# Token tiles transposed by DMA as 16-bit planes in a gated cross-attention and feed-forward kernel

## The reference

```python
x = x + tanh(g_xattn) * xattn(layernorm(x), ctx_768, mask)     # x: (2, 2048, 512), ctx: (2, 77, 384)
x = x + tanh(g_ffn) * ffn(layernorm(x))

def xattn(x, context, mask):       # 16 heads of 32
    q, k, v = x @ Wq, context @ Wk, context @ Wv
    attn = softmax(where(mask, q k^T * 32**-0.5, -max))
    return (attn @ v) @ Wo

def ffn(x):                        # int8 fake quantisation, hidden size 1408
    xq = fake_quant(x)             # one scale from max |x| over the whole tensor
    h = fake_quant(silu(xq @ q(w_gate)^T) * (xq @ q(w_up)^T))
    return h @ q(w_down)^T
```

## Time and profile before

| | |
|---|---|
| median of 3 runs | 651.23 us (651.05 to 651.66) |
| profiled execution | 651.6 us, span of its instructions 649.6 us |
| mean granted TensorE clock | 0.994 |
| TensorE busy | 629.0 us (97%) |
| VectorE busy | 505.3 us (78%) |
| ScalarE busy | 319.8 us (49%) |
| GpSimd busy | 174.5 us (27%) |
| first `scores` of slot 3 / of slot 28 | 60.0 us / 347.4 us after the span's start |

### The profile page before, as it was taken

How to read it: one execution, slowest core, us unless ns; L and a number is a source line. 1 busy time by engine, 2 the same in 40 slices (tenths; PEclk the granted TensorE clock), 3 DMA queues, 4 the chain that set the end, 5 groups by cost and what they waited for, 6 DMA issues and landing times. The chain is left out here.

```text
span 649.6 us, 12819 instructions
## 1 busy us (share of the span) xinstructions
PE 629.0 (97%) x3987; PEld 478.6 (74%) x4008; DVE 505.3 (78%) x954; ACT 319.8 (49%) x488; POOL 174.5 (27%) x392
## 2 busy tenths in 40 slices
PE   8969999999999999999999997899999999899997
PEld 6769999999999999999999997444444444344544
DVE  6686878788787887888888766688888888876764
ACT  4354544445444554544544432555555554365653
POOL 7121223223232222212212111111111110047775
PEclk9999999999999999999999999899999999999999
DMA  8639111101111011011112000058465110089723
GB/s 308 189 95 318 47 28 26 49 24 48 24 29 44 25 48 25 28 52 62 29 47 68 18 7 0 18 174 192 161 210 202 31 28 17 0 291 413 292 105 128
DMA packets 59861, 63.32 MB, mean 97 GB/s; under 512 B 39571, under 2 KB 42029, under 8 KB 59821
## 3 DMA queue, kind: packets, MB, share of 16 engines
q1 hardware_dynamic: 54915, 46.03, 23.7%
q10 hardware_dynamic: 4906, 16.78, 7.0%
HBM read 32.48 MB, written 21.36 MB: 83 GB/s over the span
## 5 line engine op out<-in xcount | busy, mean ns | idle before, releaser
L633 DVE TENSOR_REDUCE sb_smax<-ps_s 128x8 f32<-128x616 f32 x64 | 51.1, 799 | 59.4 <-PE ps_s L926 59.0
L1231 ACT ACTIVATE sb_silu<-ps_g,sb_sgu 128x512 f32<-128x512 f32 x88 | 60.5, 687 | 72.1 <-PE ps_g L1318 43.8
L1318 PE MATMUL ps_g<-sb_xqT,sb_wgu 128*128 128x512 bf16 x344 | 89.3, 379 | 1.0 <-DVE sb_xqT L1274 0.6
L1318 PE MATMUL ps_u<-sb_xqT,sb_wgu 128*128 128x512 bf16 x346 | 89.4, 379 | 0.3
L527 ACT COPY sb_pT<-ps_p 128x512 f32<-128x512 f32 (+1 forms) x96 | 46.5, 520 | 71.5 <-PE ps_p L937 71.5
L1289 DVE SCALAR_TENSOR_TENSOR sb_h<-ps_u,sb_sgu,sb_silu 128x512 f32<-128x512 f32 (+1 forms) x88 | 66.1, 751 | 19.4 <-PE ps_u L1318 18.8
L948 PE MATMUL ps_o<-sb_vblk,sb_pT 128*128 (+4 forms) x640 | 79.0, 270 | 1.2 <-ACT sb_pT L527 1.2
L948 PEld LDWEIGHTS ps_o<-sb_vblk,sb_pT 128*128 128x128 f32 (+1 forms) x640 | 76.8, 191 | 1.8 <-ACT sb_pT L527 1.4
L881 PE MATMUL ps_q<-sb_xT_hi,sb_wq_hi 128*128 128x256 f32 x256 | 78.0, 305 | 0.0
L882 PE MATMUL ps_q<-sb_xT_lo,sb_wq_hi 128*128 128x256 f32 x256 | 72.6, 284 | 0.0
L883 PE MATMUL ps_q<-sb_xT_hi,sb_wq_lo 128*128 128x256 f32 x256 | 72.6, 284 | 0.0
(11 more groups left out here) (212 smaller groups left out, 1351.8 us busy)
## 6 DMA issues: line engine op xcount, KB each, us to landing
h_spill<-sb_h SPq DMA_DIRECT2D x4, 2816.0 KB, 8.9
sb_h<-h_spill ACTq DMA_DIRECT2D x16, 704.0 KB, 7.5
out_dram<-sb_wgu SPq DMA_DIRECT2D x31, 256.0 KB, 2.1
sb_x<-in_x_dram ACTq DMA_DIRECT2D x1, 4096.0 KB, 16.8
sb_w_in<-in_L_ffn_w_gate_dram SPq DMA_DIRECT2D x11, 256.0 KB, 2.6
sb_w_in<-in_L_ffn_w_up_dram SPq DMA_DIRECT2D x11, 256.0 KB, 2.6
sb_x<-in_x_dram SPq DMA_DIRECT2D x2, 1024.0 KB, 14.7
sb_x<-in_x_dram SPq DMA_DIRECT2D x2, 512.0 KB, 5.3
```

Source lines behind the costliest of these rows:

```text
L633: dve.tensor_reduce(smax[:, half, :].rearrange("p (g h) -> p g h", g=2), half_scores(), X, ALU.max).then_inc(v_max, 1)
L1231: act.activation(silu[(j * KI + i) % 2][:, :, :].rearrange("p t n -> p (t n)"), p_g[(j * KI + i) % 2][:, :], ACT.Silu, scale=sgu[:, i:i + ...
L1318: last = pe.matmul(banks[(j * KI + i) % 2][:, :], wgu[:, what, k, i * P:(i + 1) * P], xqT[j][:, k, :], start=(k == 0), stop=(k == KD - 1))
```

## The change

For tiles 4 to 31 TensorE no longer transposes the token tile. The fp32 tile `xn` is seen as pairs of 16-bit halves. GpSimd copies it to `xpl` as two planes, all low halves and then all high halves (`x_split`); SP transposes the 128 x 1,024 plane tile by DMA back into `xn` (`planes_transposed`); ScalarE joins the halves into fp32 values in `xpl` and copies those to `xT_hi` (`x_join`); GpSimd writes `xpl - xT_hi` to `xT_lo` (`x_low`). Tiles 0 to 3 keep the old way. `xpl` takes the room of `xabs`; the absolute values of tiles 0 to 23 are written to the PSUM tile `p_y` in place of it, so `project` waits for their reduction, and that reduction moves ahead of the second score subtraction. `outputs_norm(n - 1, 1)` comes after two waits that stood behind it. `DIRECT` is 4, `PLANES_FREE` is 28.

```diff
 # SP
+                    def planes_transposed(n):
+                        sp.wait_ge(g_xpl, n - DIRECT + 1)
+                        sp.dma_start_transpose(xn_u[:, :].rearrange("p (c n) -> p c n", n=P),
+                                               xpl_u[:, :]).then_inc(d_xT, 16)
...
                     values_spread(0, spread)
+                    planes_transposed(DIRECT)
                     rows(1)
                     for w in range(2, NW):
                         rows_transposed(w - 2)
+                        planes_transposed(w + DIRECT - 1)
                         rows(w)
...
                     down_rows(0)
+                    planes_transposed(NW + DIRECT)
                     for r in range(KD):
+                        if WD0 + 2 * r + 1 + DIRECT < NT:
+                            planes_transposed(WD0 + 2 * r + 1 + DIRECT)
                         for q in range(WC - 1):
                             down_stored(r, q)
                         if r + 1 < KD:
                             down_rows(r + 1)
+                        if WD0 + 2 * r + 2 + DIRECT < NT:
+                            planes_transposed(WD0 + 2 * r + 2 + DIRECT)
                         down_stored(r, WC - 1)
 # GpSimd
+                    def x_split():
+                        pool.tensor_copy(xpl_planes, xn_pairs).then_inc(g_xpl, 1)
...
+                        if split:
+                            wait(pool, a_xn, n)
+                            wait(pool, v_xlo, n - 1)
+                        else:
+                            wait(pool, a_xn, n - 1)
                         pool.tensor_tensor(ve[:, :], mv[:, 1:2], eps[:, :], ALU.add).then_inc(g_self, 1)
                         pool.tensor_tensor(nmean[:, :], mv[:, 0:1], minus[:, :], ALU.mult).then_inc(g_self, 1)
+                        if split:
+                            x_split()
...
+                        if runs(n + DIRECT, NT):
+                            x_low(n + DIRECT, t)
+
+                    def x_low(n, t):
+                        wait(pool, a_xhi, n + 1)
+                        wait(pool, t_q, n - t % 2 - 2)
+                        cols = slice(t % 2 * P, (t % 2 + 1) * P)
+                        pool.tensor_tensor(xT_lo[t // 2][:, :, cols], xpl_T, xT_hi[t // 2][:, :, cols].bitcast(F32),
+                                           ALU.subtract).then_inc(v_xlo, 1)
 # ScalarE
+                    def x_join(n, t):
+                        wait(act, d_xT, (n - DIRECT) * 16 + 16)
+                        act.copy(xpl_pairs, xn_planes).then_inc(a_xpl, 1)
+                        wait(act, a_xpl, n - DIRECT + 1)
+                        wait(act, t_q, n - t % 2 - 2)
+                        act.copy(xT_hi[t // 2][:, :, t % 2 * P:(t % 2 + 1) * P], xpl_T).then_inc(a_xhi, 1)
...
-                        if runs(n + 4, NT):
-                            x_part(n + 4, t)
+                        if runs(n + DIRECT, NT):
+                            x_join(n + DIRECT, t)
 # VectorE
                         down_part(n, 1)
+                        if runs(n - 4, NT):
+                            wait(dve, a_abs, n - 3)
+                            dve.tensor_reduce(xmax[:, span(n - 4)], xabs(n - 4), X, ALU.max).then_inc(v_xmax, 1)
                         if runs(n, NT):
                             scores_sub(n, t, 1)
...
-                        if runs(n + 4, NT):
-                            x_part(n + 4, t)
 # TensorE
                         wait(pe, v_x1, m)
+                        if not isinstance(m, int) or m < PLANES_FREE - 2:
+                            wait(pe, v_xmax, m)
...
-                        if runs(n + 4, NT):
-                            wait(pe, v_olo, n - 1)
-                            x_transpose(n + 4)
```

More of the change, by code:

```diff
@@ L11 @@
 U8 = mybir.dt.uint8
+U16 = mybir.dt.uint16
 ACT = mybir.ActivationFunctionType
@@ L63, in wd_step @@
     return (r, k) if 0 <= r < KD else (None, None)
+DIRECT = 4
+PLANES_FREE = NT - DIRECT
 CHUNKS = [(0, 4), (4, 8), (8, 2 * KB)]
@@ L129, in flamingo_block @@
                 sg_1 = sb("sg_1", [P, 2])
-                xn = sb("xn", [P, D])
+                xn_u = sb("xn", [P, 2 * D], U16)
+                xn = xn_u[:, :].bitcast(F32)
                 prob = [sb(f"prob{i}", [P, 2, HW]) for i in range(2)]
@@ L141, in flamingo_block @@
                 ends_n = sb("ends_n", [P, 2, 2])
-                xabs = sb("xabs", [P, D])
+                xpl_u = sb("xpl", [P, 2 * D], U16)
+                xpl = xpl_u[:, :].bitcast(F32)
                 mv1 = [sb(f"mv1{i}", [P, 2]) for i in range(2)]
@@ L172, in flamingo_block, with xabs @@
                 p_y = pb("y", [P, D])
+                xn_pairs = xn_u[:, :].rearrange("p (n two) -> p two n", two=2)
+                xn_planes = xn_u[:, :].rearrange("p (two n) -> p two n", two=2)
+                xpl_planes = xpl_u[:, :].rearrange("p (two n) -> p two n", two=2)
+                xpl_pairs = xpl_u[:, :].rearrange("p (n two) -> p two n", two=2)
+                xpl_T = xpl[:, :].rearrange("p (k n) -> p k n", k=KD)
+                def xabs(m):
+                    return xpl[:, :] if isinstance(m, int) and m >= PLANES_FREE - DIRECT else p_y[:, :]
                 LATE = NT - 2 * (KC + KD)
@@ L292, in flamingo_block @@
                 a_xn = sem("a_xn")
+                g_xpl = sem("g_xpl")
+                d_xT = sem("d_xT")
+                a_xpl = sem("a_xpl")
                 g_wbf = sem("g_wbf")
@@ L393, in _ @@
                     rows_transposed(NW - 2)
+                    planes_transposed(NW + DIRECT - 1)
                     rows_transposed(NW - 1)
@@ L422, in _, with deviation @@
                 def _(pool):
-                    def deviation(n, t):
+                    def x_split():
+                        pool.tensor_copy(xpl_planes, xn_pairs).then_inc(g_xpl, 1)
+                    def deviation(n, t, split=False):
                         mv, rs, nb = mv1[t % 2], rs1[t % 2], nb1[t % 2]
@@ L427, in deviation @@
                         wait(pool, g_nb, n)
-                        wait(pool, a_xn, n - 1)
+                        if split:
[3 more added lines that the diff above has]
+                            wait(pool, a_xn, n - 1)
                         pool.tensor_tensor(ve[:, :], mv[:, 1:2], eps[:, :], ALU.add).then_inc(g_self, 1)
                         pool.tensor_tensor(nmean[:, :], mv[:, 0:1], minus[:, :], ALU.mult).then_inc(g_self, 1)
+                        if split:
+                            x_split()
                         wait(pool, g_self, 3 * n + 2)
@@ L449, in slot @@
                         if runs(n + 5, NT):
-                            deviation(n + 5, t + 5)
+                            deviation(n + 5, t + 5, split=True)
+                        elif runs(n + DIRECT, NT):
+                            wait(pool, a_xn, n + DIRECT + 1)
+                            wait(pool, v_xlo, n + DIRECT)
+                            x_split()
                         if runs(n - 3, NT):
@@ L495, in normalise @@
                         wait(act, g_nb, n + 1)
-                        wait(act, t_x, n)
+                        if isinstance(n, int) and n <= DIRECT:
+                            wait(act, t_x, n)
+                        else:
+                            wait(act, a_xpl, n - DIRECT)
                         act.activation(xn[:, :], x1[:, span(n), :].rearrange("p a d -> p (a d)"), ACT.Identity,
@@ L521, in slot @@
                                 wait(act, v_xmax, n - 3)
-                                act.activation(xabs[:, :], row(n - 4), ACT.Abs, bias=nb2[:, span(n - 4)],
+                                if isinstance(n, int) and n >= PLANES_FREE:
+                                    act.wait_ge(v_xlo, NT)
+                                else:
+                                    wait(act, v_x1, n - 2)
+                                act.activation(xabs(n - 4), row(n - 4), ACT.Abs, bias=nb2[:, span(n - 4)],
                                                scale=rs2[:, span(n - 4)]).then_inc(a_abs, 1)
@@ L706, in last_row @@
                         dve.wait_ge(a_abs, m)
-                        dve.tensor_reduce(xmax[:, m - 1:m], xabs[:, :], X, ALU.max).then_inc(v_xmax, 1)
+                        dve.tensor_reduce(xmax[:, m - 1:m], xabs(m - 1), X, ALU.max).then_inc(v_xmax, 1)
                         for i, op in enumerate((ALU.max, ALU.min)):
@@ L779, in slot @@
                                               ALU.subtract).then_inc(v_wo, 1)
-                        if runs(n - 4, NT):
-                            wait(dve, a_abs, n - 3)
-                            dve.tensor_reduce(xmax[:, span(n - 4)], xabs[:, :], X, ALU.max).then_inc(v_xmax, 1)
                         down_part(n, 2)
@@ L798, in slot @@
                             stats(n + 6)
-                        if runs(n - 1, NT):
-                            outputs_norm(n - 1, 1)
                         if runs(n + 6, NT):
@@ L803, in slot @@
```

(7 more changed lines are left out.)

## The result

The changed kernel takes 655.55 us (median of 5 runs, 654.00 to 655.85); the kernel before, run beside it, 651.23 (5 runs, 649.42 to 652.22). The ratio is 1.0065, 95% interval 1.0050 to 1.0079: slower by 0.65%, 4.3 us. The profiled execution took 655.55 us, its span is 653.7 (before 649.6).

The account below looks back on a forecast made before the run. TensorE was taken to bound the kernel from slot 3 on, with waits in slots 0 to 2 passed on whole. Start +10.7 us and transposes -9.2 gave +1.5 on 651.2, so 652.7 us, range 645.5 to 659.

Parts of the forecast that it names:

- Removed transposes: TensorE loses four x transposes in 28 slots; 25 slots count at 0.37 us each, a gain of 9.2 us.
- The relief of VectorE and the move to GpSimd: Full slots: VectorE's saved 0.68 us worth nothing; GpSimd's subtraction, carried at 1.3 and 1.8 us, hidden.
- The new operations: Full slots: split, plane transpose, join, copy and subtraction loop in 8.2 to 8.7 us, under 11.13, so hidden.
- Rival three: Full slots: strided 16-bit copies at half rate or GpSimd held up by VectorE; slower, 658 or 667 us; chance 0.18.
- First stall: Slots 0 and 1: tile 4's join delays ScalarE's queue; TensorE 3.8 us late, 5.4 with the clock.
- Second stall: Slots 2 and 3: tile 6's planes held to the 4 MB load's end; 9.1 us late including the first stall, 10.7 with clock.
- Rival one: Slots 2 and 3: tile 6's planes not held up by the whole load, no second stall; 647.4 us; chance 0.27.
- The clock: After each start pause TensorE runs at half clock, 3.2 us at half speed, costing 1.6 us.
- Rivals two and four: Two: start costs 1 to 3 us, 643 to 645.5, chance 0.07; four: start cancels the gain, nothing measurable, 0.06.

Follow-up runs that it names:

- e5: e3 with four identity transposes that nothing reads put back on TensorE in every slot from 0 to 27; 652.44 us.
- e7: e3 with the low part subtracted by VectorE instead of GpSimd; 643.37 us.
- e2: The changed kernel with the 4 MB and 1 MB x loads issued as five loads of 1 MB, one in each of slots 1 to 5; 644.86 us.
- e1: The changed kernel with ScalarE's copy of Wo moved ahead of the join of tile 4 in slot 0; 651.51 us.
- e9: The changed kernel with 13 and 27 identity matmuls on TensorE ahead of the first outputs of slots 1 and 3; 651.37 us.
- e3: The changed kernel with the edits of e1 and e2 together; 642.24 us, ratio 0.9864 to the kernel before.
- e6: The changed kernel with 28 and 56 identity matmuls on TensorE ahead of the first outputs of slots 1 and 3; 658.96 us.

## Why the prediction came out as it did

The forecast was two stalls at the start that cost a little more than the transposes give: 652.7 us, range 645.5 to 659. The kernel is slower, at 655.55 us inside the range, and the runs show both stalls and the gain of the full slots. The size was less good: the sum was +1.5 us and is +4.1 on the span. The term that was mis-sized is the clock.

- **Removed transposes**: 0.37 us a slot predicted, 0.39 measured, 9.3 us in the 24 full slots; e5 puts them back and loses 9.5 us there.
- **The relief of VectorE and the move to GpSimd**: nothing either way predicted, and e7 shows it. GpSimd's subtraction takes 1.28 us, the lower of the two ends carried, against 0.68 on VectorE and 0.69 in e7. (The Trainium skill, "GPSIMD Engine Reference", Engine selection, calls GpSimd about twice as slow on two-input work; 1.28 against 0.68 agrees. As a verdict on the edit it did not hold, since neither engine is the bound.)
- **The new operations**: split 1.04 us (1.2 predicted), plane transposes 3.1 (3.1), copy 0.62 (0.6). The join is 1.34 against 1.04. (The 0.83 ns an element behind the 1.04 is in no row; 1.89 us for 2,048 and 0.57 for 512 give 0.86 ns and 1.0 us. It makes no difference.) Rival three falls: the strided join is slower than its row, but the loop fits, and TensorE waits in no full slot.
- **First stall**: `outputs(0, 0)` 3.8 us late predicted; 42.16 against 38.91 is 3.25. Tile 4's planes went out at 33.48 and not at 34.34, since SP reached the value DMAs 0.9 us earlier, and the join, 0.3 us longer than predicted, gave part of it back. The pause is 3.48 us, not 5.0, because TensorE came to it late itself, at half clock from 35.5 to 38.5. The prediction has no such stretch. It begins 1.8 us after a pause of 2.17 us that ends at 33.73; in the kernel before and in e5, where four transposes still stand ahead of it, that pause is 1.73 and 1.74 us, and the clock stays at 1.00. In e2 the pause is 2.20 us and ends at 34.53, the clock stays at 1.00 in 36 to 40 us, and the pause ahead of the outputs is 4.54 us. e1 takes most of the stall away.
- **Second stall**: load issued at 51.69 (51.0 predicted), planes issued at 55.02 (about 55), join at 69.14 (68.8), `outputs(2, 0)` at 73.33 (72.7). Rival one, planes that pass the load, falls: they land after 14.1 us, 0.3 us behind the load, and after 3.4 in e2. (The Trainium skill, "DMA: Bandwidth & Descriptors", Queues, rings and completion order, has the engines change rings at packets of 9 to 17 descriptors. The prediction's estimate of 0.5 us by that rule counted a turn of the load as a single packet of the profile. If a turn of either queue is as long, the rule gives one to one, and the 951 against 951 packets agree; how long a turn is, no row here shows.) The pause is 6.96 us instead of 3.7, since TensorE came to it earlier: slot 2 took 62.62 - 51.11 = 11.5 us, in the kernel before 60.00 - 46.04 = 14.0, and slot 3 started only 2.6 us late, not 5. Of the slot's 2.5 us 1.5 are the half clock that the kernel before had there and the changed one has not, 0.6 its wait for `xT_lo` in `p_x` (0.57 at 47.73, gone with the transposes), 0.4 the transposes. The prediction passed the whole first stall on to slot 3 and was wrong in that. It did not move the forecast's time, as the end of the load sets the end of this pause.
- **The clock**: 1.6 us predicted behind a pause, from the one case of 3.2 us at half speed. The half clock lasted 6.2 and 5.9 us here and cost about 3 us each time. At the second stall, which decides, that is 1.3 to 1.4 us more than predicted. e9 holds the clock up and takes 4.2 us less.
- **Rivals two and four** fall with the 12.3 us that the start costs.

Added up at slot 4: predicted 10.7 - 0.4 = 10.3 us late, measured 12.3. Of the 2.0 between them 1.4 are the clock behind the second pause and 0.6 are outputs that start later. These 0.6 hold errors that cancel in part, which is luck: the load is issued 0.7 later (the half clock behind the first pause costs 1.4 more, the first stall 0.55 less), it takes 0.3 longer, the join takes 0.3 longer, but the planes land 0.7 closer behind the load.

The full slots then give 0.4 more than predicted: slot 28 is 3.0 us late. The last 1.1 us come behind the attention stage. Up to a pause of 1.84 us that both kernels have there (569.61, before 566.93) the changed one is 2.7 us late, and at the end 4.1: its clock is 0.81 in 566 to 574 us, where the kernel before has 1.00 in the same stretch and in 563 to 571. No instruction there is changed. Of the nine other profiled executions that have the edit, e3's alone has such a stretch (busy time by stretch in e3):

```profile
556.00:560.00 4.00, 3.49 (x13) 2.60 (x14) 3.43 (x14) 0.77 (x2) 0.00 (x0) 0.64 0.00 0
```

So it does not follow from the edit by itself. How often it comes in executions that were not profiled is not known: the five of the changed kernel have mean clocks of 0.978 to 0.979, and of 0.986 in the fastest, 654.00 us. What brings it on stays open.

## What to carry to other kernels

Price a removed TensorE instruction by a slot of the same trace that already lacks it; where TensorE is the bound, as in the full slots here, that was right to 0.02 us a slot. Then walk the first slots in each engine's own order, for there a new path has no lead: ask what stands behind the new wait in its list, and which large transfer its DMA meets. Here the price of both was above the gain, and one moved copy and a load in five pieces turned +0.65% into -1.36%.

## What the runs showed of the hardware

- A transposing DMA beside a 4 MB load on another queue was held up to the load's end: 14.1 us instead of 3.1, with one packet of 256 bytes for one of 2 KB (951 against 951 in 60 to 66 us). Beside loads of 1 MB it took at most 4.6 us; the largest with no such load beside it was 5.0.
- The half clock behind a pause of 3.5 and of 7.0 us lasted 6.2 and 5.9 us in the changed kernel, against 3.2 behind a pause of 4.41 and 3.4 in slot 2 of the kernel before. Behind a pause of 2.2 us at the end of slot 0 the clock fell to 0.50 in the changed kernel, e1, e3, e6 and e9, where the pause ended at 33.7 to 33.9 us, and stayed at 1.00 in e2 and e7, where it ended at 34.5.
- ScalarE joined 1,024 strided 16-bit halves in 1.34 us, where its fp32 rows give about 1.0; GpSimd split as many in 1.04.
- An fp32 matmul against the identity is two instructions in the trace, 0.23 us, where the kernel's fp32 transpose is one.
